# Output projection of a fused recurrent-mixing and feed-forward block: fp16 halves with power-of-two scales in place of float32r halves

## What is computed

```python
# first half; LN is layer norm without weights, eps 1e-5
xn = LN(x)
uv = xn @ in_proj_w + in_proj_b; u, v = uv[:, :512], silu(uv[:, 512:])
vl = depthwise_conv3(v, conv_w) + conv_b          # along the rows
h_t = a * h_(t-1) + ssm_b * vl_t                  # a = sigmoid(logit_a)
y_t = ssm_c * h_t + ssm_d * vl_t
g = u * silu(y)
o = g @ out_proj_w + out_proj_b                   # the output projection
x = x + LN(LN_w(o + xn))                          # LN_w has weight and bias
# second half; W1 and W2 ternary: -1, 0 or 1 by a threshold
h = gelu(LN(x) @ ternary(W1).T + b1)
x = x + LN(h @ ternary(W2).T + b2)
```

## Time and profile before

| | us |
|---|---|
| three runs, median (lowest to highest) | 1481.2 (1478.92 to 1481.64) |
| the profiled execution, its own time | 1482.46 |
| its span, first to last instruction | 1480.7 |
| PE busy in the span | 1431.2 |

### The profile page before, as it was taken

The page is one execution under the profiler, slowest core; times in us unless marked ns, Lnnn a source line. Parts: engine busy times, 40 slices in busy tenths (PEclk is TensorE's granted clock), DMA queues, the critical chain, the costliest instruction groups (busy, mean ns, idle before and its releaser), DMA issues. The chain is left out here.

```text
span 1480.7 us, 18927 instructions
## 1 busy us (share of the span) xinstructions
PE 1431.2 (97%) x6509; PEld 709.1 (48%) x6509; DVE 1113.8 (75%) x1871; ACT 866.8 (59%) x1256; POOL 420.4 (28%) x493
## 2 busy tenths in 40 slices
PE   6979989999999999999999999999999999999997
PEld 4434535445454454545445454544545454455443
DVE  7779677796867778686787867779686777998634
ACT  6676565565656655565675646556564665653543
POOL 1124213142331513232051422414242141422211
...
GB/s 266 180 74 36 64 36 86 29 58 29 86 29 29 83 17 73 29 55 60 29 68 18 86 30 39 75 29 57 29 86 29 29 86 26 32 1 29 57 29 29
DMA packets 155519, 81.99 MB, mean 55 GB/s; under 512 B 132768, under 2 KB 132768, under 8 KB 155296
## 3 DMA queue, kind: packets, MB, share of 16 engines
...
...
## 5 line engine op out<-in xcount | busy, mean ns | idle before, releaser
L559 PE MATMUL f2b<-w,ring 128*128 128x512 fp8e5 x1008 | 382.5, 379 | 4.5 <-DVE ring L696 2.6
L560 PE MATMUL f2b<-w,ring 128*128 128x512 fp8e5 x1008 | 382.2, 379 | 0.0
L531 PE MATMUL f1b<-x3T,w 128*128 128x512 f16 x960 | 367.5, 383 | 6.6 <-DMA x3T<-tp 4.8
L532 PE MATMUL f1b<-x3T,w 128*128 128x512 f16 x960 | 367.0, 382 | 0.0
L1153 ACT ACTIVATE ring<-f1b,par 128x512 f32<-128x512 f32 x256 | 174.8, 683 | 226.4 <-PE f1b L532 226.0
L1443 POOL TENSOR_SCALAR ve<-mv 128x4 f32<-128x4 f32 (+2 forms) x85 | 30.5, 359 | 774.5 <-DVE mv L688 774.3
L696 DVE SCALAR_TENSOR_TENSOR ring<-ring,f_sc 128x512 f16<-128x512 f32 x256 | 208.6, 829 | 51.8 <-ACT ring L1163 51.8
L1163 ACT ACTIVATE ring<-ring,f_sc 128x512 f16<-128x512 f32 x256 | 180.3, 710 | 0.0
L482 PE MATMUL misc<-x1T,win_hi 128*128 128x512 f16 x464 | 176.1, 380 | 3.8 <-ACT vb L1270 2.4
L484 PE MATMUL misc<-x1T,win_lo 128*128 128x512 f16 x464 | 176.0, 379 | 0.0
L483 PE MATMUL misc<-x1T,win_hi 128*128 128x512 f16 x464 | 176.0, 379 | 0.0
...
## 6 DMA issues: line engine op xcount, KB each, us to landing
...
x1T<-tp SPq DMA_TRANSPOSE x68, 3.0
...
```

The source lines that it names most:

```text
L531: pe.matmul(b[:, :], w, src[:, k, :], start=k == 0, stop=False)
L532: mm = pe.matmul(b[:, :], w, src[:, KC + k, :], start=False, stop=k == KC - 1)
L559: pe.matmul(f2b[q][:, :], h_hi[:, i % H_SLOTS, qs], w2[:, j, :], start=j == 0, stop=False)
L560: mm = pe.matmul(f2b[q][:, :], h_lo[:, i % H_SLOTS, qs], w2[:, j, :], start=False, stop=j == FC - 1)
```

## The change

The four operands of the output projection become fp16. Fp16 has a narrow range, so both operands are scaled by powers of two that are bounded on the chip: POOL works out, per feature, a bound of |g| from the parameters (`weight_bound`, nine small instructions; `gate_bound`, eight), DVE turns it into the scale `g_sc` and its counterpart for the weights (`gate_scale`, `wo_scale`; the second needs the sum of squares of the weight, which ACT's `wo_square` and PE's `wo_sum` give), and `h_add` multiplies by `o_inv`. `g_hi` and `g_lo` take a scale per partition. `stage` gets memory of its own, and its two loads wait for nothing. In the start, the weight's split, W1's sums and the threshold move to later places on ACT, DVE and PE, and the statistics of tile 2 and the first work on tile 1's v to others. The sums of W2 change their order. The core of the diff:

```diff
-        wo_hi = sb("wo_hi", [P, KC, D], F32R)
-        wo_lo = sb("wo_lo", [P, KC, D], F32R)
+        wo_hi = sb("wo_hi", [P, KC, D], F16)
+        wo_lo = sb("wo_lo", [P, KC, D], F16)
...
-        with nc.sbuf_tensor("stage", [P, 2 * KC, TT], F32) as stage:
-            pass
-        g_hi = sb("g_hi", [P, KC, TT], F32R)
-        g_lo = sb("g_lo", [P, KC, TT], F32R)
+        stage = sb("stage", [P, 2 * KC, TT])
+        g_hi = sb("g_hi", [P, KC, TT], F16)
+        g_lo = sb("g_lo", [P, KC, TT], F16)
...
-            return (f1b[0], f2b[KC - 1])[m][:, 0:1]
+            return (f2b[1], f2b[KC - 1])[m][:, 0:1]
+
+        def wo_sum_bank():
+
+            return f2b[KC - 1][:, 0:1]
...
-                else:
-                    sp.wait_ge(o_mm, NB)
                 sp.dma_start(w2_raw[group], w2_d[group]).then_inc(w2_in[group], 16)
...
-            load_w2(3)
-            load_w2(0)
-            transposes("t1", 2)
             load_w2(1)
             load_w2(2)
+            load_w2(0)
+            load_w2(3)
+            transposes("t1", 2)
...
+                if (kind, t, i) == ("u", 0, KC - 1):
+                    pe.wait_ge(wo_sc_ok, 1)
...
-                pe.wait_ge(thr_ok, 2)
                 for j in range(NB):
+                    if j == NB - 1:
+                        pe.wait_ge(thr_ok, 2)
...
-                pe.wait_ge(v_ok, KC + 1 if m == 0 else 3 * KC)
+                pe.wait_ge(v_ok, 2 * KC if m == 0 else 3 * KC)
                 pe.wait_ge(thr_ok, 2 * m + 1)
                 pe.matmul(thr_bank(m), ones[:, :], thr_s[:, m:m + 1], start=True, stop=True).then_inc(thr_mm, 1)
...
+            def wo_sum():
+
+                pe.wait_ge(v_ok, KC)
+                pe.wait_ge(wo_ss_ok, 1)
+                pe.matmul(wo_sum_bank(), ones[:, :], wq[:, 1:2], start=True, stop=True).then_inc(wo_mm, 1)
...
                 in_proj("v", 1, b, v_mm)
-            threshold(0)
+                if b == 1:
+                    wo_sum()
             in_proj("u", 0, 2, u_mm)
             in_proj("u", 0, 3, u_mm)
+            threshold(0)
             o_first()
...
             def gate_lo(c, b):
                 ve_.wait_ge(ghi_ok, KC * c + b + 1)
-                if c == 1 and b == 0:
-                    ve_.wait_ge(w_ok, N_KEPT)
-                ve_.tensor_tensor(g_lo[:, b, :], yb[:, b, :], g_hi[:, b, :].bitcast(F32),
-                                  ALU.subtract).then_inc(glo_ok, 1)
+                ve_.scalar_tensor_tensor(out=g_lo[:, b, :], in0=yb[:, b, :], scalar=g_sc[:, b:b + 1], in1=g_hi[:, b, :],
+                                         op0=ALU.mult, op1=ALU.subtract).then_inc(glo_ok, 1)
...
-                ve_.scalar_tensor_tensor(out=dst, in0=bank("o", c, j)[:, :], scalar=inv_sig[:, 0:1],
+                ve_.scalar_tensor_tensor(out=dst, in0=bank("o", c, j)[:, :], scalar=o_inv[:, 0:1],
                                          in1=dst, op0=ALU.mult, op1=ALU.add).then_inc(h_ok, 1)
...
+            def gate_scale():
+
+                ve_.wait_ge(bnd_ok, 1)
+                link(ve_.tensor_scalar(bnd[:, 5, :].bitcast(U32), bnd[:, 4, :].bitcast(U32), 0x7F800000, None, ALU.bitwise_and))
+                link(ve_.tensor_scalar(g_inv[:, :], bnd[:, 5, :], 2.0 ** -25, None, ALU.mult))
+                link(ve_.tensor_scalar(bnd[:, 5, :], bnd[:, 5, :], 2.0 ** -3, None, ALU.mult))
+                ve_.reciprocal(g_sc[:, :], bnd[:, 5, :]).then_inc(g_sc_ok, 1)
+                link(ve_.tensor_reduce(wq[:, 0:1], g_inv[:, :], AX.X, ALU.max))
+                ve_.wait_ge(wo_sq_ok, 1)
+                ve_.tensor_scalar(wq[:, 1:2], wo_sq[:, :], wq[:, 0:1], wq[:, 0:1], ALU.mult, ALU.mult).then_inc(wo_ss_ok, 1)
+
+            def wo_scale():
+
+                ve_.wait_ge(wo_mm, 1)
+                link(ve_.tensor_scalar(wq[:, 2:3], wo_sum_bank(), 2.0 ** -100, None, ALU.max))
+                link(ve_.tensor_scalar(wq[:, 3:4].bitcast(U32), wq[:, 2:3].bitcast(U32), 1, 0x7F800000,
+                                       ALU.logical_shift_right, ALU.bitwise_and))
+                link(ve_.tensor_scalar(wq[:, 4:5], wq[:, 3:4], 2.0 ** 50, None, ALU.mult))
+                link(ve_.reciprocal(wq[:, 5:6], wq[:, 4:5]))
+                link(ve_.tensor_scalar(wo_sc[:, :], g_inv[:, :], wq[:, 5:6], None, ALU.mult))
+                link(ve_.tensor_scalar(o_inv[:, :], wq[:, 4:5], inv_sig[:, 0:1], 2.0 ** 22, ALU.mult, ALU.mult))
+                ve_.reciprocal(o_sc[:, :], o_inv[:, :]).then_inc(wo_sc_ok, 1)
...
             def setup_out_proj(k):
                 ve_.wait_ge(wo_h, k + 1)
-                ve_.tensor_tensor(wo_lo[:, k, :], wo_raw[:, k, :], wo_hi[:, k, :].bitcast(F32),
-                                  ALU.subtract).then_inc(wo_l, 1)
+                ve_.scalar_tensor_tensor(out=wo_lo[:, k, :], in0=wo_raw[:, k, :], scalar=wo_sc[:, k:k + 1],
+                                         in1=wo_hi[:, k, :], op0=ALU.mult, op1=ALU.subtract).then_inc(wo_l, 1)
...
             setup_scales()
-            setup_out_proj(0)
-            t_lo("t1", 1, 0)
-            setup_out_proj(1)
-            t_lo("t1", 1, 1)
-            setup_out_proj(2)
-            t_lo("t1", 1, 2)
-            setup_out_proj(3)
-            t_lo("t1", 1, 3)
+            for j in range(NB):
+                t_lo("t1", 1, j)
             abs_sum(0)
             taps(0, 0, True)
             taps(0, 1, True)
+            gate_scale()
             abs_sum(1)
-            run(ln1(2))
             taps(0, 2, True)
             taps(0, 3, True)
+            x_stats(2, 0)
+            x_stats(2, 1)
             taps(0, 0, False)
+            wo_scale()
             scan(0, 0)
             y(0, 0)
             taps(0, 1, False)
-            threshold_sum(0)
+            x_stats(2, 2)
+            x_stats(2, 3)
+            for j in range(NB):
+                aggr(0, 2, j)
             scan(0, 1)
+            setup_out_proj(0)
+            setup_out_proj(1)
             taps(0, 2, False)
             y(0, 1)
-            threshold(0)
+            threshold_sum(0)
+            setup_out_proj(2)
+            setup_out_proj(3)
             ve_.wait_ge(par_ok, 8)
...
+            threshold(0)
...
-                if b == 0 and c == 1:
-                    act.wait_ge(w_ok, place[W2_CHUNK, 7] + 1)
-                act.activation(g_hi[:, b, :], yb[:, b, :], ACT.Copy).then_inc(ghi_ok, 1)
+                elif b == 0:
+                    act.wait_ge(g_sc_ok, 1)
+                act.activation(g_hi[:, b, :], yb[:, b, :], ACT.Copy, scale=g_sc[:, b:b + 1]).then_inc(ghi_ok, 1)
...
                 act.wait_ge(row_in, 16)
-                act.wait_ge(prep, 4)
-                act.activation(xn[0:1, :], ob_row[0:1, :], ACT.Copy, scale=sig[0:1, 0:1]).then_inc(ob_ok, 1)
+                act.wait_ge(wo_sc_ok, 1)
+                act.activation(xn[0:1, :], ob_row[0:1, :], ACT.Copy, scale=o_sc[0:1, 0:1]).then_inc(ob_ok, 1)
...
                 act.wait_ge(loaded, 16)
+                if n == 0:
+                    act.wait_ge(wo_sq_ok, 1)
...
+            def wo_square():
+
+                act.wait_ge(wout_in, 16)
+                act.activation(w2[:, 0:KC, :].rearrange("p c n -> p (c n)"), wo_raw.rearrange("p k n -> p (k n)"), ACT.Square,
+                               accum_out=wo_sq[:, 0:1], saturate=False).then_inc(wo_sq_ok, 1)
...
             def split_out(k):
-                act.wait_ge(wout_in, 16)
-                act.activation(wo_hi[:, k, :], wo_raw[:, k, :], ACT.Copy).then_inc(wo_h, 1)
+
+                act.wait_ge(wo_sc_ok, 1)
+                act.activation(wo_hi[:, k, :], wo_raw[:, k, :], ACT.Copy, scale=wo_sc[:, k:k + 1]).then_inc(wo_h, 1)
...
+            act.activation(pa[:, :], par[:, 0:LA + 4 * KC], ACT.Abs).then_inc(pabs_ok, 1)
...
-            for k in range(KC):
-                split_out(k)
+            wo_square()
...
-            abs_sum(0, 3, w1_raw[3], w1_in[3])
-            out_bias()
             silu_v(1, 0)
             d_conv(0, 0)
             silu_v(1, 1)
+            abs_sum(0, 3, w1_raw[3], w1_in[3])
+            d_conv(0, 1)
+            silu_v(1, 2)
+            silu_y(0, 0)
+            silu_v(1, 3)
+            split_out(0)
+            split_out(1)
+            d_conv(0, 2)
+            split_out(2)
+            split_out(3)
+            out_bias()
+            silu_y(0, 1)
             abs_sum(1, 2, w1_raw[2], w1_in[2])
-            silu_y(0, 0)
-            silu_v(1, 2)
-            d_conv(0, 1)
-            silu_v(1, 3)
-            d_conv(0, 2)
-            silu_y(0, 1)
...
-            abs_sum(2, 4, w2_raw[0], w2_in[0])
-            abs_sum(3, 7, w2_raw[3], w2_in[3])
+            abs_sum(2, 5, w2_raw[1], w2_in[1])
+            abs_sum(3, 6, w2_raw[2], w2_in[2])
             for b in range(KC):
                 centre_tap(1, b)
-            abs_sum(4, 5, w2_raw[1], w2_in[1])
-            abs_sum(5, 6, w2_raw[2], w2_in[2])
+            abs_sum(4, 4, w2_raw[0], w2_in[0])
+            abs_sum(5, 7, w2_raw[3], w2_in[3])
...
```

(36 more changed lines are left out.)

15 lines of the change are left out of this document (added).

## The result

The changed kernel took 1472.85 us, median of 4 runs (1472.04 to 1474.28); the kernel before 1481.42 beside it (1478.92 to 1483.73). The ratio is 0.9944, 95% interval 0.9925 to 0.9962: faster by 0.4 to 0.75%. The forecast was 1472.2, with 1467 to 1479. The profiled execution took 1474.28 with a span of 1472.5 us, 8.2 under the 1480.7 of before.

The account below looks back on a forecast made before the run. PE's matmuls were taken to bound the steady part, waits the start. Steady terms -10.1 + 0.3 - 0.4 - 0.2 = -10.4 us, plus 1.4 at the start, gave -9.0: from 1481.2 to 1472.2 us, range 1467 to 1479.

Parts of the forecast that it names:

- longer chains: Gate chains to h_add: scaled g_lo and g_hi add about 0.2 us, 0.3 in tile 14; covered in steady tiles.
- the start: Stretch up to f1(0): the new order, with its later sum and threshold, gives back 1.4 us; bounds -1.5 and +6.
- 2.44 us that it took for the loads: PE's wait for ACT at u(1): early W2 loads save all 2.44 us of it.
- The steady part: Out-projection blocks of tiles 2 to 13: fp16 saves 0.84 us per tile on PE, 10.1 us in all.
- tile 1: Out-projection block: first 24 matmuls gain nothing, the others 0.4, less 0.2 for the chain: 0.2 us gained.
- tile 15: Out-projection block: 24 matmuls come after 1356.21 and gain 0.4 us.
- Tile 14: Chain through DVE: PE's 0.84 us turns into idle time, and longer g_lo and g_hi add about 0.3 us.
- Two steps inside o_first: First fp16 matmul at about 65.5 us, and 2.5 us added for the lower clock; end at 78.4.
- the lower clock in o_first: PE at 1.2 GHz in o_first after the idle gap before threshold(0), taken as 2.5 us.
- Rival 1: PE idles over 3 us before v(2), which starts at 1.2 GHz: +1.7 to +3.4, 1474 to 1476; chance 0.19.
- Rivals 2 and 3: Start no slower or a little faster, 1469 to 1471 (0.12); start eats nearly all the gain, 1477 to 1481 (0.07).
- rivals 4 and 5: Type does not make the pace, 1482.6 (0.03); TensorE at 1.2 GHz from 54 us to threshold(1), 1493 (0.05).

Follow-up runs that it names:

- e5: The kernel before with only the four output-projection tensors fp16, constant scale for g, output wrong in size, order and loads unchanged: 1469.07 us.
- e6: e4's kernel with the four tensors float32r again and stage sharing the gates' memory as before: 1485.60 us.
- e4: The changed kernel with the two early W2 loads waiting for o_first again and ACT's W2 sums in their old order: 1473.21 us.
- e9: The changed kernel unaltered, run and profiled a second time: 1472.25 us.
- e3: The changed kernel with 34 added matmuls on PE before threshold(0), to fill its idle gap: 1472.38 us.
- e10: Changed kernel with ACT's second W1 sum and threshold(1) earlier, dummy matmuls around tile 0's transposes, plus ACT's bias row ahead of the weight splits: 1464.65 us.

## Why the prediction was right, and how far its terms hold

The total was right within 1 us, the direction and the mechanism too. Of its two parts the runs say this. By the medians of e5 and e6 the type gave 12.1 to 12.4 us, where the forecast's steps, without its longer chains, sum to 10.9 (10.1, and 0.4 each in tiles 1 and 15). The rest cost 3.8 to 4.4, where the forecast has 1.9 (1.4 at the start, 0.5 for the chains). But 1.0 to 1.3 us of the type's gain come there through the W2 loads that wait for o_first. In the changed kernel they wait for nothing, and the forecast had this in the 2.44 us that it took for the loads. Without it the type stands at some 11.1 us against 10.9, and the rest at 2.8 (by e5) or some 2.0 (by e6, less the 1.1 of e4 too) against 1.9. These are estimates from medians and single profiles, and the times alone can't tell them from the forecast (the interval of e5 is 9.9 to 13.9). No term is shown to be off by more than that. That the sum came within 1 us is in part luck, since the clock alone moves a profile by 1.7 us (e9).

**The steady part** was right by its own steps. fp16 takes 0.2157 us in this place: block 10.57, -10.2 over the twelve steps against -10.1; e5 and e6 show it from both sides. In e5, where no scale lengthens the chain, the blocks of tile 1 and tile 15, taken from the matmul ahead, gain 0.4 (16.73 to 16.34 us) and 0.5 (12.32 to 11.81), the 0.4 and 0.4 of the forecast before its chain terms. With the 1.0 us between v(2) and f1(0) that makes some 12.2; the median has 12.1. `g_lo` took 741 ns (744 taken) and `g_hi` 721, 0.09 over its old 629 (0.08 taken). The forecast took `g_lo` from line 900 as a whole; e5 and e6 show which part of that form costs: the scale per partition. The chain that got longer stayed under cover: the first h_add of tile 3, here in the DVE timeline, ends at 342.80, 0.75 us before the 25th matmul wants its bank, where I had 0.8.

```profile
342.06 0.74 DVE L832 SCALAR_TENSOR_TENSOR hb<-misc,o_inv,hb 128x512 f32<-128x512 f32 x1
```

The rule of the Trainium skill (TensorE: Matmul & The Clock Gate, section "Wait — 56ns, not 53.3ns?"), N / 2.4 GHz + 2.5 ns with no type named, fits the fp16 and fp8 rows at the full clock here (0.2157 us). The float32r blocks of before and of e6, 0.84 us longer, don't follow it.

**Tile 14** lost 0.2 (0.3 forecast) and **tile 15** gained 0.4 (0.4) by the table, but 0.2 when taken from the matmul ahead. In tile 14 a short wait for h_add came up inside the block, which I had not named. It is 0.21 us in the PE timeline, and the two starts around it stand 0.59 apart, not 0.22:

```profile
1299.67 0.39 PE L508 MATMUL misc<-wo_hi,g_hi 128*128 128x512 f16 x1 [0.21 <-DVE hb L832]
```

**Tile 1** gained nothing, where I had 0.2: PE waited 4.11 us for h_add(1, 0) and not 3.50, and more of the block ran at 1.2 GHz (10 starts 0.43 us apart, before 7). That is within what the clock does from one execution to the next.

**The start** cost 1.8 us at f1(0) in the first profile (0.7 in e9's), 1.4 forecast. By the median of e5 all but the type costs 3.8 us. The 1.0 of the loads is in it, and 0.5 for the scales' longer operations at tiles 14 and 15; what the other 2 us are isn't settled. Between the profiles of e5 and e9, 3.1 us apart, the step from tile 1's block to tile 2's holds 2.3 us, with 7 and 18 starts 0.43 us apart; e5 has one profile, so whether the program or chance makes its clock is open. Its steps on ACT and DVE, timeline of each:

```profile
41.49 0.78 ACT L1320 ACTIVATE vb<-f1b,par,inv_sig 128x512 f32<-128x512 f32 x1 [2.04 <-PE f1b L499]
...
56.58 1.89 ACT L1330 ACTIVATE w<-xs 128x2048 fp8e5<-128x2048 f32 x1
```
```profile
58.60 0.16 DVE L979 TENSOR_REDUCE thr_s<-asum 128x1 f32<-128x4 f32 x1 [4.37 <-ACT w L1330]
...
59.99 0.75 DVE L811 SCALAR_TENSOR_TENSOR yb<-misc,bu_sig,yb 128x512 f32<-128x512 f32 x1
...
68.77 1.53 DVE L816 SCALAR_TENSOR_TENSOR g_lo<-yb,g_sc,g_hi 128x512 f16<-128x512 f32 x2
...
76.91 0.69 DVE L824 SCALAR_TENSOR_TENSOR tp<-yb,tp 128x512 f16<-128x512 f32 x1
```

Forecast against measured: silu of v(1, 0) 40.7 and 41.5; the second sum's end 58.0 and 58.5; PE idle 4.2 and 4.4; gate(0, 0) 59.5 and 60.0; the last g_lo's end 69.9 and 70.3; last t_lo 76.5 to 77.2 and 76.9; v(2) 80.5 and 81.05; threshold(1) 96.2 and 96.6; f1(0) 108.2 and 108.6. Two steps inside o_first were off and cancelled. The k-loop began at 66.8 and not at 65.5, as the last bias matmul started at 64.81 (64.2 forecast) and took 2.0 us; and only six of its steps ran at the lower clock, 1.3 us and not 2.5. Its end, 78.4, was right only by that; the sum doesn't hang on it, since v(2) was laid on the transposes.

**Two readings** in the forecast were loose. I put the 2.44 us that PE had waited at u(1) down to late loads and counted them as saved; from v(2) to f1(0) the change does save 2.6 us (30.11 to 27.52), but e4 shows that the loads are worth 1.1 of them. And it took the lower clock in o_first for the gap's alone: the kernel before and e3 have it behind the bias matmuls (see e3).

**The rivals.** Rival 1 (a gap ahead of v(2) drops the clock) did not happen in the changed kernel, after 2.29 us, nor in e3 after 3.12; it did in e10 after 2.96 (six matmuls). Rivals 2 and 3 put the start too low and too high; rivals 4 and 5 fell, by e6 and by a granted clock of 0.80 in the stretch from 50 to 76 us, as before.

So the start took back a good part of the gain: the type alone stands at 1469.07, the change at 1472.85 or 1472.25, and with the sum in a better place the same type and scales at 1467.66.
